# Two cross-attention layers on TensorE: the products for the running maxima issued as row tiles of 64 and of 32 rows

## The chip, the cores and the metric

The kernel runs on one core of one Trainium2 chip. Each time below is device time in microseconds (us) from one execution of the whole program; the metric is the median over runs. There is one profiled execution, and the trace belongs to it.

## The reference, cut to what matters

The program computes a small two-layer network on x (2 x 256 tokens, 256 wide) with a context of 2 x 4096 rows, 256 wide. Each layer is cross-attention over the context, a second mixer, and a feed-forward part with experts. The change touches the two cross-attentions alone:

```python
# layer 0: 8 heads of 64; layer 1: 16 heads of 16, with biases on q, k, v
q = (layernorm(x) @ Wq).reshape(b, n, HEADS, DIM_HEAD)
k = (context @ Wk).reshape(b, m, HEADS, DIM_HEAD)
v = (context @ Wv).reshape(b, m, HEADS, DIM_HEAD)
attn = softmax(q k^T * scale, axis=-1)      # over all 4096 rows of the context
x = x + (attn @ v) @ Wo + bo
```

A softmax needs a shift per query and head. The kernel takes the largest product over all 4096 keys, so it multiplies queries by keys twice: once with queries down the partitions, to reduce along the free axis to a maximum ("maxima"), and later once more with keys down the partitions, with the shift folded in, to take exponentials ("scores"). Any shift close to the maximum serves, since it cancels in the quotient.

## The kernel before, in words

**Units and chunks.** Both layers (`cross0` and `cross1`, each a function in every engine's program) work through 4 units: batch 0 or 1 times the first or second half of the heads. A unit holds 4 heads in layer 0 (`HPU0`) and 8 heads in layer 1 (`HPU1`). The 4096 rows of context are 8 chunks of 512 (`NCH`), so there are 32 chunks g in all. At step t of 41 the kernel makes keys and values of chunk t, maxima of chunk t - 1, and scores, exponentials and mixture of chunk t - 9 (`LAG` = 9, a whole unit and one step later, because the shift must be known). So steps 1 to 8 have maxima and no scores, steps 9 to 32 have both, and steps 33 to 40 have scores alone. The order on TensorE (PE) is written out by hand: for each head or block n of a step, `scores(g, n)`, then `maxima(t - 1, n)`, then the pieces that the step's plan puts there: `mixture` (attention weights times values), `keys` and `values`. PE runs its queue in order.

**Layer 1's plan (`slots_of`, L236).** There are 8 slots n in a step. In units 1 and 3 (steps 9 to 15 and 24 to 31, all but the first of the second stretch) two keys products each stand behind slots 1, 3 and 4 and the mixture behind slots 0, 2, 5 and 7; nothing stands behind slot 6 but the next scores. In unit 2 (steps 16 to 23) two keys products stand behind slot 1 and four behind slot 3, values behind 5 and 7, and the mixture behind 0, 2, 4 and 6. Step 24 and step 32 have the mixture behind 0, 2, 4 and 6 and nothing behind the odd slots.

**Layer 0's order (L1399).** Head h: `scores(g, h)` is 8 products of 256 columns, then `maxima(t - 1, h)`; behind the four heads stand keys, `mixture(g, 0)`, `mixture(g, 1)`, values and the turning of the context.

**Maxima (L1319 and L1525).** A call makes two products of 128 x 512 in fp32r for one head h: the head's queries (first 128, then last 128) are the weights, and 512 keys stream past. In layer 0 the weights are `qh0`, which holds the rounded queries twice, in partitions 0 to 63 and 64 to 127; the keys `k0` of an even head hold the rounded part in partitions 0 to 63 and the remainder in 64 to 127, an odd head the other way round. One product of 128 rows thus multiplies the queries by the whole key. In layer 1 the weights are the unit's queries masked to one head (16 rows of 128 are not zero) and `ef1` holds the rounded keys of all 8 heads of the unit.

**Where the products go.** In steps 1 to 8 (`early`) both go to one `score` tensor, two banks of PSUM, and VectorE (DVE) reduces both in one instruction (`reduce_early`, L2050). From step 9 on they go to single banks that `place_free` (L1268) hands out after waiting for the last reader, and DVE reduces each with an instruction of its own (L2085, L2210). Layer 0 rotates through three banks (`order0`, `place0`). Layer 1 has two for this: product n goes to ring place 1 + n % 2, so that product n waits for the reduction of product n - 2. `ms` counts the products done and `red` the reductions done.

**Tiles of columns.** Two existing lines issue column tiles: the mixture of layer 0 (L1344, `tile_position=(0, 64 * j)`, 64 columns of weights) and that of layer 1 (L1552, `(0, 32 * j)`, 17 columns of weights in a tile of 32). Each fp32 product there shows as two matmuls in the trace. All the other products of the two layers' loops use the array whole. No instruction of the kernel before uses a tile of rows.

The lines of the old maxima loop in layer 1, in which the wait for a bank stands ahead of each single product:

```python
for q in range(2):
    dst = score[h % 2][:, 512 * q:512 * q + 512] if early else place_free(a, g + 1, f"m{2 * h + q}")[:]
    mm(dst, masked_queries1(u)[:, h, 128 * q:128 * q + 128], ef1[:, g % ERING, 0, :], start=True, stop=True).then_inc(a["ms"], 1)
```

Of the kernel before, what the change touches and what calls it, by code (L numbers as in the profile page):

```python
# [64 lines left out]
def perceiver(nc, ins, out):  # L65
    ctx = ExitStack()
    with ctx:
# [160 lines left out]
        def masked_queries1(u):  # L228

            return qm1[:] if u % 2 == 0 else qm1b[:, :, 256:512]  # L230
# [50 lines left out]
        def bank_of(a, t, use):  # L281
            return ring[place_of(a, t, use)]
# [957 lines left out]
        def _(pe):  # L1240
# [59 lines left out]
            def cross0():  # L1300
# [17 lines left out]

                def maxima(g, h):  # L1319
                    u, i = divmod(g, NCH)  # L1320
                    if i == 0:
                        pe.wait_ge(a["qh"], a.n("qh", 8 * u + 2 * h + 2))
                    if h % 2 == 0:
                        pe.wait_ge(a["kl"], a.n("kl", 2 * g + h // 2 + 1))
                    early = g + 1 < LAG
                    if early and 4 * g + h >= 2:
                        pe.wait_ge(a["red"], a.n("red", 8 * g + 2 * h - 2))
                    for q in range(2):
                        dst = score[h % 2][:, 512 * q:512 * q + 512] if early else place_free(a, g + 1, f"m{2 * h + q}")[:]
                        mm(dst, qh0[:, u % 3, h, 128 * q:128 * q + 128], k0[:, g % LAG, h, :], start=True, stop=True).then_inc(a["ms"], 1)  # L1330

                def mixture(g, n):
                    u, i = divmod(g, NCH)
# [149 lines left out]
            def cross1():  # L1483
# [40 lines left out]

                def maxima(g, h):  # L1525
                    u, i = divmod(g, NCH)
                    if i == 0:
                        pe.wait_ge(a["qh"], a.n("qh", 8 * u + h + 1))
                    if h == 0:
                        pe.wait_ge(a["kh"], a.n("kh", g + 1))  # L1530
                    early = g + 1 < LAG
                    if early and 8 * g + h >= 2:
                        pe.wait_ge(a["red"], a.n("red", 16 * g + 2 * h - 2))
                    for q in range(2):
                        dst = score[h % 2][:, 512 * q:512 * q + 512] if early else place_free(a, g + 1, f"m{2 * h + q}")[:]
                        mm(dst, masked_queries1(u)[:, h, 128 * q:128 * q + 128], ef1[:, g % ERING, 0, :], start=True, stop=True).then_inc(a["ms"], 1)  # L1536

                def mixture(g, blocks):
                    u, i = divmod(g, NCH)
# [461 lines left out]
        def _(dve):  # L2001
# [42 lines left out]
                dve.wait_ge(a["ch"], a.n("ch", 2 * half_index(g) + f + 1))  # L2044
                v.tensor_tensor(lo[:, f, :], bank_of(a, g - 1, f"t{f}")[:], hi[:, f, :].bitcast(F32), ALU.subtract).then_inc(a["cl"], 1)

            def reduce_early(a, mx, per_chunk, g, h):

                dve.wait_ge(a["ms"], a.n("ms", per_chunk * g + 2 * h + 2))
                v.tensor_reduce(mx[:, 0, g, 2 * h:2 * h + 2], score[h % 2][:].rearrange("p (q k) -> p q k", q=2), AX.X, ALU.max).then_inc(a["red"], 2)  # L2050

            def low_weights(setup, n, lo, src, hi):

# [23 lines left out]
            def cross0():  # L2077
                a = a0

                def reduce(g, h):  # L2080
                    u, i = divmod(g, NCH)
                    for q in range(2):
                        n = 2 * h + q
                        dve.wait_ge(a["ms"], a.n("ms", 8 * g + n + 1))
                        v.tensor_reduce(mx0[:, u % 2, i, n:n + 1], bank_of(a, g + 1, f"m{n}")[:], AX.X, ALU.max).then_inc(a["red"], 1)  # L2085

                def maximum(u):
                    dve.wait_ge(a["red"], a.n("red", 8 * NCH * (u + 1)))
# [51 lines left out]
                for t in range(STEPS):  # L2140
                    g = t - LAG
                    for h in range(HPU0):
                        if LAG <= t <= CHUNKS:
                            reduce(t - 1, h)
                        if 1 <= t < LAG:
                            reduce_early(a, mx0, 8, t - 1, h)
                        if t < NCH and h in (1, 2):
                            low_keys(t, h - 1)
                    if t % NCH == 0 and 0 < t <= CHUNKS:
                        maximum(t // NCH - 1)  # L2150
                    if NCH <= t < CHUNKS:
                        low_keys(t, 0)
                        low_keys(t, 1)
                    if g > 0 and g % NCH == 0:
                        divide(a, g // NCH - 1, oT0, den0[:]).then_inc(a["o"], 1)
                    if g == CHUNKS - 1:
                        for h in (1, 2, 3):
                            last_sums(h)
                    elif g >= 0:
                        sums(g)  # L2160
                    if is_turned(t + 1):
                        context_of(t + 1)
                    if t % NCH in (1, 2, 3, 4) and t < CHUNKS:
                        low_queries(t // NCH, t % NCH - 1)
# [15 lines left out]
            def cross1():  # L2180
# [24 lines left out]
                def reduce(g, h):  # L2205
                    u, i = divmod(g, NCH)
                    for q in range(2):
                        n = 2 * h + q
                        dve.wait_ge(a["ms"], a.n("ms", 16 * g + n + 1))
                        v.tensor_reduce(mx1[:, u % 2, i, n:n + 1], bank_of(a, g + 1, f"m{n}")[:], AX.X, ALU.max).then_inc(a["red"], 1)  # L2210

                def maximum(u):
                    dve.wait_ge(a["red"], a.n("red", 16 * NCH * (u + 1)))
# [44 lines left out]
                for t in range(STEPS):  # L2258
                    g = t - LAG
                    u, i = divmod(t, NCH)  # L2260
                    for h in range(HPU1):
                        if LAG <= t <= CHUNKS:
                            reduce(t - 1, h)
                        if 1 <= t < LAG:
                            reduce_early(a, mx1, 16, t - 1, h)
                        if (t < NCH and h == 1) or ((i or u % 2 == 0) and LAG <= t < CHUNKS and h == slots_of(t)[2] + 1):
                            low_keys(t)
                        if g > NCH and t < CHUNKS:
                            finish_part(g // NCH - 1, g % NCH, h)
                    if i == 0 and 0 < t <= CHUNKS:  # L2270
                        maximum(u - 1)
                    if i == 0 and u % 2 and NCH <= t < CHUNKS:
                        low_keys(t)
                    if g > 0 and g % NCH == 0 and t > CHUNKS:
                        finish(g // NCH - 1)
                    if u and i in (1, 2, 3, 4) and t < CHUNKS:
                        low_queries(u, 2 * i - 2)
                        low_queries(u, 2 * i - 1)
                    if t == CHUNKS + 3:
                        dve.wait_ge(rw["y"], 1)  # L2280
                        v.tensor_scalar(rw_rest[:], rw_vec[:, 2:5, :], -1.0, 1.0, ALU.mult, ALU.add)
                        v.tensor_scalar(rw_wexp[:], rw_wexp[:], -1.0, None, ALU.mult).then_inc(rw["mx"], 1)
                    if CHUNKS + 2 < t < CHUNKS + 7:
                        n = t - CHUNKS - 3
                        dve.wait_ge(rw["tr"], n + 1)
                        v.tensor_copy(rw_W[:, n], bank[0][:].rearrange("p (f n) -> p f n", f=2)).then_inc(rw["trc"], 1)
# [352 lines left out]
```

## Time and profile before

| what | value |
|---|---|
| median of 3 runs | 1577.31 us (1574.79 to 1585.05) |
| the profiled execution: its own time | 1577.6 us |
| its span, first to last instruction | 1575.7 us |
| mean granted TensorE clock | 0.984 of full |
| PE busy | 1493.4 us, 95% |
| DVE busy | 1007.7 us, 64% |
| ACT busy | 757.7 us, 48% |
| POOL busy | 545.3 us, 35% |

Busy time of an engine is the time in which at least one of its instructions ran. PE's matmuls overlap in the trace, and the ends are modelled, so what one of them costs in a stream is the distance between starts, not its duration. PEld is the loading of weights, which can run beside a matmul.

### The profile page before, as it was taken

The numbers are of one execution on the slowest core, as the hardware profiler recorded it, in microseconds if no ns is written. First come the engines' busy times: TensorE is split into PE (matmuls) and PEld (weight loads), VectorE is DVE, ScalarE is ACT, GpSimd is POOL, SyncE is SP. The second block draws the span as 40 slices with busy tenths as digits, with TensorE's granted clock in tenths as the row PEclk, the third lists the DMA queues.
The fourth block names the chain that finished last, engine by engine and source line by source line (L and its number), as shares of the span: only waits on it lengthen the run. The fifth ranks groups of instructions, "written<-read, shape, count | busy, mean of one in ns | idle before, by whom it ended". The sixth has DMA issues, their size and how long they took to land.

```text
span 1575.7 us, 26268 instructions
## 1 busy us (share of the span) xinstructions
PE 1493.4 (95%) x10057; PEld 1102.0 (70%) x10057; DVE 1007.7 (64%) x1568; ACT 757.7 (48%) x1027; POOL 545.3 (35%) x688
## 2 busy tenths in 40 slices
PE   7999999999998998899999887999999999998898
PEld 6877877877886757689998664555666555444498
DVE  6976567666654367576766888876876887206711
ACT  5645555554544425443442223555555555785131
POOL 1015443452547930000000622753554554670000
PEclk9999999999999999799999999999999999999899
DMA  5433333332324200023223223211111220000354
GB/s 187 161 127 101 124 118 108 130 111 81 121 81 108 55 29 1 22 87 107 81 83 103 81 106 107 81 54 55 71 64 55 81 81 1 2 2 1 107 179 154
DMA packets 68817, 134.27 MB, mean 85 GB/s; under 512 B 9010, under 2 KB 39268, under 8 KB 68708
## 3 DMA queue, kind: packets, MB, share of 16 engines
q1 hardware_dynamic: 68516, 132.74, 25.8%
q8 instruction: 72, 1.18, 0.3%
q14 instruction: 37, 0.30, 0.1%
q10 hardware_dynamic: 192, 0.05, 0.0%
HBM read 98.64 MB, written 17.30 MB: 74 GB/s over the span
## 4 chain that ended last, share of the span: by engine, by line
PE 81%; DVE 9%; POOL 3%; ACT 2%; issue 2%; DMA 1%; SPq 1%; ACTq 0%; DVEq 0%; POOLq 0%
PE bank L1278 14%; PE score L1521 8%; PE bank L1552 8%; PE bank L1536 6%; PE bank L1842 6%; PE score L1278 6%; PE bank L1344 5%; PE bank L1330 3%; PE score L1315 3%; PE bank L1565 2%; PE score L1316 2%; DVE mx L2210 2%; DVE mx L2050 2%; PE bank L1926 2%; PE bank L1936 2%
## 5 line engine op out<-in xcount | busy, mean ns | idle before, releaser
L992 ACT ACTIVATE P<-score 128x1024 f32<-128x1024 f32 x256 | 256.5, 1024 | 145.2 <-PE score L1521 145.0
L727 POOL CAST st<-ef 32x512 fp32r<-32x512 f32 x384 | 234.9, 612 | 242.4 <-PE score L1521 197.4
L2210 DVE TENSOR_REDUCE mx<-bank 128x1 f32<-128x512 f32 x384 | 246.8, 685 | 88.5 <-PE bank L1536 84.7
L1521 PE MATMUL score<-qs,st 97*128 97x512 f32 x512 | 172.9, 426 | 3.7 <-DMA qs<-shift 2.4
L686 POOL TENSOR_TENSOR sum<-sum,P 128x512 f32<-128x512 f32 x82 | 108.5, 1324 | 185.6 <-ACT P L897 185.6
L2085 DVE TENSOR_REDUCE mx<-bank 128x1 f32<-128x512 f32 x192 | 123.7, 686 | 69.4 <-PE bank L1330 60.7
L897 ACT ACTIVATE P<-score 128x1024 f32<-128x1024 f32 x128 | 129.6, 1026 | 69.3 <-PE score L1316 67.0
L1552 PE MATMUL bank<-P,v 128*17 128x256 f32 x2048 | 134.4, 382 | 0.0
L1315 PE MATMUL score<-qh,k 128*128 128x256 f32 x512 | 130.3, 288 | 4.4 <-ACT P L897 2.3
L1521 PEld LDWEIGHTS score<-qs,st 97*128 97x128 f32 x512 | 84.3, 189 | 69.6 <-ACT P L992 36.2
L1278 PE MATMUL bank<-w_split,c_hi 128*128 128x256 f32 x688 | 128.9, 287 | 2.5 <-DVE k L2097 1.7
L1316 PE MATMUL score<-ql,w 65*128 65x256 f32 x512 | 127.9, 283 | 0.0
L1344 PE MATMUL bank<-P,v 128*64 128x256 f32 x1024 | 118.1, 382 | 0.4 <-ACT P L897 0.4
L1278 PEld LDWEIGHTS bank<-w_split,c_hi 128*128 128x128 f32 x688 | 108.0, 190 | 14.9 <-issue 8.8
L2050 DVE TENSOR_REDUCE mx<-score 128x2 f32<-128x1024 f32 x96 | 112.4, 1218 | 7.7 <-PE score L1536 4.2
L688 POOL TENSOR_TENSOR sum<-sum,P 128x512 f32<-128x512 f32 x82 | 107.9, 1316 | 6.4
L1315 PEld LDWEIGHTS score<-qh,k 128*128 128x128 f32 x512 | 97.5, 190 | 13.6 <-issue 8.6
L1536 PE MATMUL bank<-ef,qm1b 128*128 128x512 f32 x256 | 96.3, 428 | 4.0 <-DVE mx L2210 1.0
L1316 PEld LDWEIGHTS score<-ql,w 65*128 65x128 f32 x512 | 97.7, 191 | 3.2
L1344 PEld LDWEIGHTS bank<-P,v 128*64 128x64 f32 x1024 | 70.4, 137 | 42.1 <-issue 7.0
L907 ACT ACTIVATE v<-bank 128x512 f32<-128x512 f32 x64 | 38.3, 599 | 122.6 <-PE bank L1278 121.2
L1278 PE MATMUL bank<-w_split,c_lo 128*128 128x256 f32 x344 | 97.1, 282 | 0.0
(415 smaller groups left out, 2834.6 us busy)
## 6 DMA issues: line engine op xcount, KB each, us to landing
c_hi<-split_ctx SPq DMA_DIRECT2D x47, 512.0 KB, 3.2
c_lo<-split_ctx SPq DMA_DIRECT2D x47, 512.0 KB, 4.2
w<-k SPq DMA_DIRECT2D x128, 128.0 KB, 3.5
arena<-in_L_ffn_W SPq DMA_DIRECT2D x16, 1024.0 KB, 5.3
c_in<-in_ctx SPq DMA_DIRECT2D x16, 512.0 KB, 3.8
w1raw<-in_L_ffn_w SPq DMA_DIRECT2D x8, 1024.0 KB, 4.9
arena<-in_L_ffn_w SPq DMA_DIRECT2D x8, 1024.0 KB, 5.4
split_ctx<-c_hi SPq DMA_DIRECT2D x12, 512.0 KB, 3.5
```

Source lines behind the costliest of these rows:

```text
L727: pool.tensor_copy(st1[32 * block:32 * block + 32, k, :], ef1[rows, g % ERING, part, :].bitcast(F32)).then_inc(a[f"st{k}"], 16)
L897: act.activation(P[:, h, :], score[h % 2][:], ACT.Exp).then_inc(a["p"], 1)
L992: act.activation(P1[:, index % PRING, :], score[n % 2][:], ACT.Exp).then_inc(a["p"], 1)
L1278: last = mm(dst, l, r, start=(n == 0), stop=(n == len(pairs) - 1))
L1315: mm(o, k0[:, g % LAG, h, keys], qh0[:, u % 3, h, :], start=True, stop=False)
L1316: last = mm(o, w0[0:65, h, keys], ql0[0:65, u % 2, h, :], start=False, stop=True)
L1344: last = mm(mix[64 * j:64 * j + 64, S * n:S * n + S], v0[:, g % LAG, k, 64 * h:64 * h + 64], P[:, h, S * k:S * k + S], start=False, stop=F ...
L1521: last = mm(score[n % 2][:, 512 * j:512 * j + 512], st1[0:97, pair, 128 * k:128 * k + 128], qs1[0:97, u % 2, 2 * pair:2 * pair + 2, :], st ...
L1536: mm(dst, masked_queries1(u)[:, h, 128 * q:128 * q + 128], ef1[:, g % ERING, 0, :], start=True, stop=True).then_inc(a["ms"], 1)
L1552: last = mm(mix[32 * j:32 * j + 17, S * quad:S * quad + S], v1[:, (NCH * (u // 2) + i) % VRING, k, h, :], P1[:, index % PRING, S * j:S * j ...
L2050: v.tensor_reduce(mx[:, 0, g, 2 * h:2 * h + 2], score[h % 2][:].rearrange("p (q k) -> p q k", q=2), AX.X, ALU.max).then_inc(a["red"], 2)
L2210: v.tensor_reduce(mx1[:, u % 2, i, n:n + 1], bank_of(a, g + 1, f"m{n}")[:], AX.X, ALU.max).then_inc(a["red"], 1)
```

## The change

In both layers a call of `maxima` no longer makes both query halves of one head with 128 rows. It makes one query half q of two heads that lie in different groups of partitions, as two row tiles, into the same two banks.

- Layer 0: call h makes half q = h % 2 of heads 2 * (h // 2) and 2 * (h // 2) + 1. Tile j takes partitions 64 j to 64 j + 63. These rows hold the rounded keys alone, so the remainder takes no part in the maxima, and the wait is for `kh` in place of `kl`.
- Layer 1: call h makes half q = h % 2 of heads `first` and `first + 2`, in tiles of 32 rows. Rows left out are zero in the masked queries.
- Both destinations are asked for before the first product, so both waits of `place_free` stand ahead of both products.
- The waits for queries `qh` at the start of a unit ask for the later of the two heads.
- The reductions are the same in number and shape; only the column of the table of maxima to which each writes is another.

```diff
@@ PE, layer 0 @@
 def maxima(g, h):
     u, i = divmod(g, NCH)
+    pair, q = divmod(h, 2)
     if i == 0:
-        pe.wait_ge(a["qh"], a.n("qh", 8 * u + 2 * h + 2))
-    if h % 2 == 0:
-        pe.wait_ge(a["kl"], a.n("kl", 2 * g + h // 2 + 1))
+        pe.wait_ge(a["qh"], a.n("qh", 8 * u + 4 * pair + 4))
+    if q == 0:
+        pe.wait_ge(a["kh"], a.n("kh", 2 * g + pair + 1))
     early = g + 1 < LAG
     if early and 4 * g + h >= 2:
         pe.wait_ge(a["red"], a.n("red", 8 * g + 2 * h - 2))
-    for q in range(2):
-        dst = score[h % 2][:, 512 * q:512 * q + 512] if early else place_free(a, g + 1, f"m{2 * h + q}")[:]
-        mm(dst, qh0[:, u % 3, h, 128 * q:128 * q + 128], k0[:, g % LAG, h, :], start=True, stop=True).then_inc(a["ms"], 1)
+    dst = [score[h % 2][:, 512 * j:512 * j + 512] if early else place_free(a, g + 1, f"m{2 * h + j}")[:] for j in range(2)]
+    for j in range(2):
+        rows = slice(64 * j, 64 * j + 64)
+        mm(dst[j], qh0[rows, u % 3, 2 * pair + j, 128 * q:128 * q + 128], k0[rows, g % LAG, 2 * pair + j, :], start=True, stop=True,
+           tile_position=(64 * j, 0)).then_inc(a["ms"], 1)
@@ PE, layer 1 @@
 def maxima(g, h):
     u, i = divmod(g, NCH)
+    first, q = 4 * (h // 4) + h // 2 % 2, h % 2
     if i == 0:
-        pe.wait_ge(a["qh"], a.n("qh", 8 * u + h + 1))
+        pe.wait_ge(a["qh"], a.n("qh", 8 * u + first + 3))
...
-    for q in range(2):
-        dst = score[h % 2][:, 512 * q:512 * q + 512] if early else place_free(a, g + 1, f"m{2 * h + q}")[:]
-        mm(dst, masked_queries1(u)[:, h, 128 * q:128 * q + 128], ef1[:, g % ERING, 0, :], start=True, stop=True).then_inc(a["ms"], 1)
+    dst = [score[h % 2][:, 512 * j:512 * j + 512] if early else place_free(a, g + 1, f"m{2 * h + j}")[:] for j in range(2)]
+    for j in range(2):
+        head = first + 2 * j
+        rows = slice(32 * (head // 2), 32 * (head // 2) + 32)
+        mm(dst[j], masked_queries1(u)[rows, head, 128 * q:128 * q + 128], ef1[rows, g % ERING, 0, :], start=True, stop=True,
+           tile_position=(32 * (head // 2), 0)).then_inc(a["ms"], 1)
@@ DVE, layer 1; layer 0 and reduce_early alike @@
-    v.tensor_reduce(mx1[:, u % 2, i, n:n + 1], bank_of(a, g + 1, f"m{n}")[:], AX.X, ALU.max).then_inc(a["red"], 1)
+    m = 2 * (4 * (h // 4) + h // 2 % 2 + 2 * q) + h % 2
+    v.tensor_reduce(mx1[:, u % 2, i, m:m + 1], bank_of(a, g + 1, f"m{n}")[:], AX.X, ALU.max).then_inc(a["red"], 1)
```

## Rows read from the trace of the kernel before

**Rows 1.** Chain of work that ended last, by engine.

```profile
PE 81%; DVE 9%; POOL 3%; ACT 2%; issue 2%; DMA 1%; SPq 1%; ACTq 0%; DVEq 0%; POOLq 0%
```

**Rows 2.** Busy time by stretch: PE, PEld, DVE, ACT, POOL; clock, DMA, GB/s.

```profile
145.00:385.00 240.00, 236.02 (x1666) 191.99 (x1665) 154.50 (x230) 128.56 (x181) 104.74 (x83) 1.00 0.37 117
...
875.00:1000.00 125.00, 106.44 (x579) 73.10 (x581) 107.44 (x117) 38.48 (x50) 48.44 (x71) 0.97 0.28 101
...
1240.00:1370.00 130.00, 125.21 (x915) 66.75 (x915) 89.70 (x144) 80.64 (x86) 72.71 (x119) 1.00 0.09 33
```

**Rows 3.** Groups by line: the whole page's L1552; L2050 from 875 to 975 us.

```profile
L1552 PE MATMUL bank<-P,v 128*17 128x256 f32 x2048 | 134.4, 382 | 0.0
...
L2050 DVE TENSOR_REDUCE mx<-score 128x2 f32<-128x1024 f32 x64 | 74.1, 1217 | 4.6 <-PE score L1536 4.2
```

**Rows 4.** Timeline, layer 1, a step of unit 3, slot 0 to slot 0 (start, us).

```profile
1301.44 0.63 PE L1536 MATMUL bank<-ef,qm1b 128*128 128x512 f32 x2
...
1301.88 2.69 DVE L2210 TENSOR_REDUCE mx<-bank 128x1 f32<-128x512 f32 x4 [0.83 <-PE bank L1536]
...
1302.84 0.89 PE L1536 MATMUL bank<-ef,qm1b 128*128 128x512 f32 x2
...
1303.22 0.19 PEld L1536 LDWEIGHTS bank<-ef,qm1b 128*128 128x128 f32 x1 [0.41 <-DVE mx L2210]
...
1305.21 0.63 PE L1536 MATMUL bank<-ef,qm1b 128*128 128x512 f32 x2
...
1308.68 1.29 DVE L2210 TENSOR_REDUCE mx<-bank 128x1 f32<-128x512 f32 x2 [0.35 <-PE bank L1536]
...
1310.38 0.63 PE L1536 MATMUL bank<-ef,qm1b 128*128 128x512 f32 x2
...
1311.55 1.10 PE L1536 MATMUL bank<-ef,qm1b 128*128 128x512 f32 x2
...
1316.26 0.63 PE L1536 MATMUL bank<-ef,qm1b 128*128 128x512 f32 x2
```

**Rows 5.** Timeline, layer 1: into the tiles of 32 columns and out again.

```profile
1101.66 0.63 PE L1536 MATMUL bank<-ef,qm 128*128 128x512 f32 x2
...
1102.22 0.13 PEld L1552 LDWEIGHTS bank<-P,v 128*17 128x17 f32 x8 [0.37 <-issue]
1102.22 0.41 PE L1552 MATMUL bank<-P,v 128*17 128x256 f32 x4
...
1102.22 0.63 PE L1552 MATMUL bank<-P,v 128*17 128x256 f32 x8
...
1103.21 0.30 PEld L1521 LDWEIGHTS score<-qs,st 97*128 97x128 f32 x2 [0.42 <-ACT P L992]
1103.21 0.73 PE L1521 MATMUL score<-qs,st 97*128 97x512 f32 x2
...
1103.78 0.63 PE L1536 MATMUL bank<-ef,qm 128*128 128x512 f32 x2
```

**Rows 6.** Timeline, PE, layer 0: tiles of 64 columns.

```profile
303.09 0.39 PE L1278 MATMUL bank<-c_hi,w_split 128*128 128x512 f32 x1
...
303.41 0.65 PE L1344 MATMUL bank<-P,v 128*64 128x256 f32 x4
...
307.01 0.50 PE L1278 MATMUL bank<-w_split,c_hi 128*128 128x256 f32 x2
```

**Rows 7.** Chain in order of time: 96 products of 256 columns.

```profile
713.32 11.52 PE bank L1842 x96
```

**Rows 8.** Timeline, PE, unit 2 of layer 1: slot 1 of two steps; step 32.

```profile
1108.26 0.83 PE L1536 MATMUL bank<-ef,qm 128*128 128x512 f32 x2
...
1125.10 0.83 PE L1536 MATMUL bank<-ef,qm 128*128 128x512 f32 x2
...
1334.83 0.62 PE L1536 MATMUL bank<-ef,qm1b 128*128 128x512 f32 x2
...
1338.59 0.63 PE L1536 MATMUL bank<-ef,qm1b 128*128 128x512 f32 x2
```

More of the change, by code:

```diff
@@ L2045, in context_low, with reduce_early @@
                 v.tensor_tensor(lo[:, f, :], bank_of(a, g - 1, f"t{f}")[:], hi[:, f, :].bitcast(F32), ALU.subtract).then_inc(a["cl"], 1)
-            def reduce_early(a, mx, per_chunk, g, h):
+            def reduce_early(a, out, per_chunk, g, h):
                 dve.wait_ge(a["ms"], a.n("ms", per_chunk * g + 2 * h + 2))
-                v.tensor_reduce(mx[:, 0, g, 2 * h:2 * h + 2], score[h % 2][:].rearrange("p (q k) -> p q k", q=2), AX.X, ALU.max).then_inc(a["red"], 2)
+                v.tensor_reduce(out, score[h % 2][:].rearrange("p (q k) -> p q k", q=2), AX.X, ALU.max).then_inc(a["red"], 2)
             def low_weights(setup, n, lo, src, hi):
@@ L2084, in reduce @@
                         dve.wait_ge(a["ms"], a.n("ms", 8 * g + n + 1))
-                        v.tensor_reduce(mx0[:, u % 2, i, n:n + 1], bank_of(a, g + 1, f"m{n}")[:], AX.X, ALU.max).then_inc(a["red"], 1)
+                        m = 4 * (h // 2) + 2 * q + h % 2
+                        v.tensor_reduce(mx0[:, u % 2, i, m:m + 1], bank_of(a, g + 1, f"m{n}")[:], AX.X, ALU.max).then_inc(a["red"], 1)
                 def maximum(u):
@@ L2145, in cross0 @@
                         if 1 <= t < LAG:
-                            reduce_early(a, mx0, 8, t - 1, h)
+                            reduce_early(a, mx0[:, 0, t - 1, 4 * (h // 2) + h % 2:4 * (h // 2) + h % 2 + 3:2], 8, t - 1, h)
                         if t < NCH and h in (1, 2):
@@ L2264, in cross1 @@
                         if 1 <= t < LAG:
-                            reduce_early(a, mx1, 16, t - 1, h)
+                            reduce_early(a, mx1[:, 0, t - 1, 8 * (h // 4) + h % 4:8 * (h // 4) + h % 4 + 5:4], 16, t - 1, h)
                         if (t < NCH and h == 1) or ((i or u % 2 == 0) and LAG <= t < CHUNKS and h == slots_of(t)[2] + 1):
```

## The prediction

> **What bounds the kernel now.** I read the chain of waits first, then busy time by stretch, then timelines of single steps. The chain is 81% PE [rows 1], and by stretch PE is busy 236.0 of 240 us in layer 0 and 125.2 of 130 us late in layer 1 at a granted clock of 1.00 [rows 2]. So what a maxima call costs on PE is paid in full. One stretch is different: steps 1 to 8 of layer 1, where DVE is busy 107.4 us and PE 106.4 us of 125 [rows 2] and 64 reductions of 1.217 us, idle 4.6 us in all, set the pace [rows 3].
>
> The timeline of layer 1 shows a second bound under PE. A step of unit 3 takes 14.82 us from slot 0 to slot 0 (1301.44 to 1316.26) [rows 4]. Its PE work, from the pieces below, is 4 slots with mixture of 2.12, three with keys of 1.41 and one bare slot of 0.94 = 13.65 us. The missing 1.17 us are waits for the maxima banks: a pair of products takes 0.63 us undisturbed, but 0.89 and 1.10 us at 1302.84 and 1311.55, because the second needs DVE's second reduction [rows 4]. Note what saves this step today: the first product starts after the *first* reduction, so that DVE finds work and runs four reductions in 2.69 us without a gap [rows 4].
>
> **Prices from rows.**
> - A 512-column product in a stream costs 0.235 us (two take 0.63 us [rows 5], and one alone lasts 0.39 [rows 6]). A call of two is 0.47. A 256-column product costs 0.12 (96 in 11.52) [rows 7].
> - Entering a mode of column tiles: two products starting at 1101.66 would let the next start at 1102.13; it starts at 1102.22 [rows 5]. In layer 0 the one at 303.09 frees PE at 303.32 and the tile starts at 303.41 [rows 6]. Both 0.09 us, and weights are not loaded ahead: PEld starts with PE and had been idle 0.37 us [rows 5].
> - Leaving: four of the layer 1 tiles start together, the next four 0.22 later (0.41 against 0.63 for 4 and 8), so 16 take 0.88; the next product starts 0.99 after the first (1102.22 to 1103.21), 0.11 more. Then the two scores take 0.57 to the next start (1103.21 to 1103.78), not 0.47: the first must wait for its 128-column weight load, 0.10 [rows 5]. In layer 0 32 matmuls take 3.60 us (303.41 to 307.01): 16 pairs at 0.215 are 3.44, about 0.05 is the first load of 64 columns, and 0.09 to 0.11 the way out; then the first two L1278, of 256 columns, last 0.50 together, about 0.10 more than 0.12 and the 0.28 that one takes alone [rows 6]. So a change of shape is 0.09 of emptying, plus the exposed load of the next weights: nothing seen for 17 columns, 0.10 for 128.
> - Tiles of different columns do overlap fully: 4 at a time, and 2 at a time, in the time of one (0.22) [rows 5, 6]. No row shows row tiles.
>
> The Trainium skill (TensorEngine Tiling, Key Properties) says that changing the tiling mode, not merely the tile, drains TensorE; the 0.09 us of [rows 5, 6] agree for columns, and nothing here shows it for rows. By that rule the sum below stands; without it the first rival does.
>
> **Part 1: the pair as row tiles.** Removed: 0.47 us. Added: the pair together. I take 0.255: one product's 0.235 and 0.02 for the second tile, since four tiles of columns together last 0.41 where one lasts 0.382 [rows 3, 5]. Bounds: 0.235 for perfect overlap, and 0.47 for none. The second load of 128 columns may queue behind the first (0.11 apart in [rows 5]: two loads in 0.30, one lasting 0.19), which makes 0.365.
>
> **Part 2: the changes of shape.** Before and after nearly every call stands work on the whole array. In: 0.09 + 0.10 for the load of 128 columns. Out: 0.09 + 0.10. Bounds for each of the two: 0 (row tiles need no emptying) and 0.21 (the dearest seen). I take the middle values, since two kinds of column tile gave the same. An isolated call is then 0.19 + 0.255 + 0.19 = 0.635 against 0.47: **+0.165**. A call in front of a mixture (layer 1, 4 of 8) already pays the step into tiles; it gains 0.19 going in and loses 0.215: 2.095 against 2.12, **-0.025**.
>
> Layer 0, steps 9 to 32: 24 x 4 isolated calls x 0.165 = +15.8. Steps 1 to 8: 32 x 0.165 = 5.3, of which I take 5. The banks do no harm there: with three of them a call waits for the first reduction of the call before, 0.44 + 0.60 + some 0.2 us after it, and calls are 1.4 us apart or more (eight score products of 0.12 and the pair). Waiting for `kh`, not `kl`, gives nothing: mixture, values and the next scores of PE (over 8 us) lie between the keys of a chunk and its maxima.
>
> **Part 3: both bank waits ahead of both products (layer 1, steps 9 to 32).** Now the next call needs both reductions. The loop is: product start to first reduction 0.44 (1301.44 to 1301.88), two reductions 1.29 (row at 1308.68; also the first two of the 2.69), release at 1303.17 to weight load 0.05 (1303.22), load to product 0.11 (the pair of 1302.84 ends at 1303.73, so its second product, 0.39 to 0.40 long, started at 1303.33) [rows 4]. Sum **1.89 us** from call to call, whatever PE could do. Before, no such floor held for one slot; only DVE's own 0.65 per reduction did. Queued behind the waiting product on PE are the next scores, and behind them ACT and the mixture. DVE's other work, one `low_keys` and the pieces of the division, fits in the 0.6 us per slot in which DVE now idles.
>
> - Units 1 and 3, 15 steps: four slots with mixture 2.095; those with two keys products 0.255 + 0.19 + 0.47 + 0.47 + 0.19 = 1.575 and the bare one 1.105, all four raised to 1.89. Sum 15.94 against 14.82: +1.12, x 15 = +16.8.
> - Unit 2, 8 steps: period 16.84 (1108.26 to 1125.10) [rows 8]. New: four of 2.095, slot 1 at 1.89, slot 3 (four keys products) 2.045, two with values 2.545 (12 products of 0.12 = 1.44) = 17.40: +0.56, x 8 = +4.5.
> - Step 32: two slots took 3.76 (1334.83 to 1338.59) [rows 8], now 2.095 + 1.89 = 3.985: x 4, +0.9.
> - Steps 1 to 8: PE has 18 us of slack in 125 [rows 2] and waits in pairs before as now; 64 x 0.165 would be 10.6 if none were covered, 0 if all. DVE's reductions idle only 4.6 us [rows 3], so I take +2.
>
> **Other edits**, all 0: the reductions' new columns are the same work; the later `qh` wait falls at a unit's start, where those queries were made during the unit before. At the first unit it could cost one cast, under 1 us.
>
> **Sum.** 15.8 + 5 + 16.8 + 4.5 + 0.9 + 2 = +45.0 us. On the profiled execution's 1577.6 that is **1622 us**; the median of the runs is 1577.3, the same to 0.02%. The likeliest case's own range: with the loads in the way in hidden (-0.10 per call outside the 1.89 us slots: 128 in layer 0, 8 x 7 and 16 x 4 in layer 1 = 248) it is 1598; with the second load behind the first (+0.11 on the same 248) 1650.
>
> **Rivals.**
> 1. *Row tiles need no emptying and their loads run ahead.* For: nothing in the trace has a row tile, and all tiles of columns overlapped. Against: both kinds of column tile were emptied before and after. A call falls by 0.215. Layer 0: 96 x 0.215 = 20.6, and 5 of the early ones. Layer 1 keeps the 1.89 floor: units 1 and 3 four slots of 1.905 and four of 1.89 = 15.18, still +0.36 x 15 = +5.4; unit 2 four of 1.905, two of 1.89, two of 2.165 = 15.73, -1.11 x 8 = -8.9. Total -29: **1548 us**. The mechanism wins on PE once emptying and exposed load together are below (0.47 - 0.255) / 2 = 0.107 us a side; the whole 29 us come only at zero.
> The Trainium skill (TensorE: Matmul & The Clock Gate, Part 3) reports row tiles starting about 4 ns apart and a 3.07-fold gain for four of them; that bears on tiles in a row of their own, as the pair, not on the way in and out, and no row here shows it.
> 2. *The tiles do not overlap* (the change then does not do what it says), with the emptying paid. For: fp32r weights of 128 columns are a kind that no tile here has. Against: the two column tile shapes. Call +0.38 isolated, +0.19 before a mixture: layer 0 +48, units 1 and 3 16.80 against 14.82 = +29.7, unit 2 18.91 = +16.6, early and step 32 +10: **1682 us**.
> 3. *Half the price*, emptying and load together 0.10 a side: layer 0 stays as it is; units 1 and 3 are four slots of 2.005 and four of 1.89 = 15.58, +11.4 in 15 steps; unit 2 is -2.8 in all: **1587 us**.
>
> **How the numbers follow.** Forecast 0.60, rival 1 0.25, rival 2 0.07, rival 3 0.08. A measurement of this kernel can tell about 1% from no change. Rival 1 is the faster side, 0.25; rival 3, 0.6% up, is mostly within 1%, 0.06; slower 0.69. The 8 in 10 range goes from 1545, which takes in the larger part of rival 1, to 1655; rival 2 and the tails are left out.
>
> **What would show it.** Right: in layer 0 the pair of maxima products starts 0.1 to 0.2 us later than a stream would have it, both within 0.03 us, and the work behind starts late as well; in units 1 and 3 of layer 1 calls in slots 1, 3, 4 and 6 stand 1.89 us apart with DVE idle some 0.6 us before each pair; a step of unit 3 is near 15.9 us and PE's busy share there falls. Wrong: a maxima pair in layer 0 followed by the next score product within 0.26 us, weights loaded ahead of the pair, or a step of layer 0 shorter than before; then rival 1 holds. Starts of the two tiles 0.235 apart would be rival 2.

## The result, and the profile after

The changed kernel takes 1701.8 us (median of 4 runs, 1677.4 to 1760.9) against 1581.2 (4 runs). The ratio of the runs, less those that a low clock lengthened most, is 1.061, interval 1.052 to 1.070. The four runs differ as their mean granted clock does: 1677.4 us at 0.937, 1678.8 at 0.934, 1724.9 at 0.900 and 1760.9 at 0.872. The profiled one is that of 1724.9 us (span 1722.9), 147.3 us longer than the profiled one of before. The forecast, 1622 us, has the sign right and falls short by far; 1701.8 lies outside its range of 1545 to 1655.

Where the time went, by three instructions that both kernels have: the idle products ahead of the second mixer of layer 0 (end of its cross-attention), those ahead of layer 1's cross-attention, and the first denominators of layer 1, which open step 33. First the kernel before, timeline of PE:

```profile
566.65 4.06 PE L1246 MATMUL score<-zeros 128*128 128x512 bf16 x18 [1.39 <-DVEq L300]
...
862.31 4.05 PE L1246 MATMUL score<-zeros 128*128 128x512 bf16 x18
...
1346.66 1.13 PE L1588 MATMUL score<-oT,den_pick 128*128 128x256 f32 x4 [1.62 <-ACT oT L1018]
```

and the changed one:

```profile
578.15 4.06 PE L1246 MATMUL score<-zeros 128*128 128x512 bf16 x18 [1.39 <-DVEq L300]
...
875.42 4.05 PE L1246 MATMUL score<-zeros 128*128 128x512 bf16 x18
...
1494.20 1.13 PE L1595 MATMUL score<-oT,den_pick 128*128 128x256 f32 x4 [1.61 <-ACT oT L1018]
```

The stretch up to the end of layer 0's cross-attention is 11.5 us longer, what lies between 1.6, and steps 0 to 32 of layer 1 take 618.8 us for 484.4: +134.4. The remaining 75.0 us to the output products are the same in both. Busy time by stretch for those steps and for the 75 us behind them, changed kernel (columns as in [rows 2]):

```profile
875.42:1494.20 618.78, 570.73 (x3084) 280.30 (x3081) 379.62 (x551) 244.30 (x275) 239.30 (x374) 0.76 0.15 55
1494.20:1569.20 75.00, 73.68 (x664) 34.06 (x664) 7.90 (x10) 62.52 (x66) 51.78 (x84) 1.00 0.01 2
```

The same steps of the kernel before:

```profile
862.31:1346.66 484.35, 457.78 (x3085) 283.99 (x3082) 377.79 (x551) 241.02 (x275) 238.85 (x374) 0.99 0.20 70
```

The number behind the five busy times, the granted clock, is the finding: it is 0.76 over the stretch with maxima, where it was 0.99 before, and 1.00 again once they are over. DVE, ACT and POOL do the same work in the same busy time; only PE is longer busy. By level: the clock is at 2.4 GHz (a granted clock of 1.00) for some stretches and at 1.2 (0.50) for others, tens of microseconds long, in the same code. A step of units 1 and 3 in either, by the starts of its calls; first at full clock (from the call behind the bare slot, slot 7, to the next one, timeline of PE):

```profile
1086.52 0.50 PE L1542 MATMUL bank<-ef,qm1b 32*128 32x512 f32 x2 [0.81 <-DVE mx L2219]
1088.61 0.50 PE L1542 MATMUL bank<-ef,qm1b 32*128 32x512 f32 x2
1090.68 0.50 PE L1542 MATMUL bank<-ef,qm1b 32*128 32x512 f32 x2
1092.65 0.50 PE L1542 MATMUL bank<-ef,qm1b 32*128 32x512 f32 x2 [0.33 <-DVE mx L2219]
1094.73 0.50 PE L1542 MATMUL bank<-ef,qm1b 32*128 32x512 f32 x2
1096.70 0.50 PE L1542 MATMUL bank<-ef,qm1b 32*128 32x512 f32 x2 [0.33 <-DVE mx L2219]
1098.64 0.49 PE L1542 MATMUL bank<-ef,qm1b 32*128 32x512 f32 x2 [0.31 <-DVE mx L2219]
...
1102.68 0.49 PE L1542 MATMUL bank<-ef,qm1b 32*128 32x512 f32 x2 [0.81 <-DVE mx L2219]
```

then at half:

```profile
1325.59 0.79 PE L1542 MATMUL bank<-ef,qm1b 32*128 32x512 f32 x2
...
1350.89 0.79 PE L1542 MATMUL bank<-ef,qm1b 32*128 32x512 f32 x2
```

16.16 us against 25.30. Answering to [rows 4], the full-clock step is 16.16 for 14.82 before, with calls 2.07 to 2.09 apart across a mixture and 1.94 to 1.97 elsewhere, the latter held by DVE's reductions: the forecast said 15.94, 2.095 and 1.89. At half clock only one of the eight calls of the step shows a wait for DVE, and 9.1 us a step are lost. An estimate of the whole: of 618.8 us, (1 - 0.76) x 2 x 618.8 = 297 ran at half; if each gives back what it does in this step, 1 - 16.16 / 25.30 = 0.36 us, that is about 107 us. Without them the stretch would be some 512 us, 27 above before.

In layer 0 the clock is 1.00, and the price of a call can be read against [rows 5, 6] (timeline, changed kernel):

```profile
302.41 0.28 PE L1316 MATMUL score<-ql,w 65*128 65x256 f32 x1
302.62 0.19 PEld L1332 LDWEIGHTS bank<-k,qh 64*128 64x128 f32 x2
302.62 0.49 PE L1332 MATMUL bank<-k,qh 64*128 64x512 f32 x2
...
303.04 0.19 PEld L1315 LDWEIGHTS score<-qh,k 128*128 128x128 f32 x1 [0.24 <-issue]
303.04 0.39 PE L1315 MATMUL score<-qh,k 128*128 128x256 f32 x1
...
303.27 0.28 PE L1316 MATMUL score<-ql,w 65*128 65x256 f32 x1
```

The score product of 302.41 would let the next start at 302.53; the two tiles start at 302.62, 0.09 late, one with the other to the two decimals shown, and both weight loads lie inside 0.19 us. The next product is issued 0.42 later and its second 0.23 after that, 0.11 late. Whole call: 303.27 - 0.12 - 302.53 = 0.62 us for 0.47, +0.15; the forecast said +0.165. So row tiles overlap fully, loads side by side, and the array is emptied before and after, as for columns. The Trainium skill's rule (TensorEngine Tiling, Key Properties), that a change of mode drains TensorE, holds here for rows too: 0.09 us going in, and about as much going out (0.42, less 0.10 for the exposed load and 0.235 for the pair).

### The profile page after: what moved, and what is told of

Same layout as the page of the kernel before. It is cut to its first block, busy times and chain, and to the rows that moved or that the text cites. A ratio compares the mean times of both kernels' runs of the same rounds, so it can differ in the third digit from the quotient of the medians.

```text
span 1722.9 us, 26466 instructions
## 1 busy us (share of the span) xinstructions
PE 1613.9 (94%) x10057; PEld 1080.1 (63%) x10057; DVE 1010.9 (59%) x1568; ACT 760.7 (44%) x1027; POOL 544.8 (32%) x688
## 4 chain that ended last, share of the span: by engine, by line
PE 79%; DVE 11%; POOL 3%; ACT 2%; issue 2%; DMA 1%; SPq 1%; ACTq 0%; DVEq 0%; POOLq 0%
PE bank L1278 13%; PE bank L1559 9%; PE score L1524 8%; PE bank L1542 6%; PE bank L1849 5%; PE score L1278 5%; PE bank L1347 5%; DVE mx L2219 4%; PE bank L1572 3%; PE score L1315 3%; PE score L1316 2%; DVE mx L2057 2%; PE bank L1332 2%; PE bank L1933 2%; PE bank L1943 2%
## 5 line engine op out<-in xcount | busy, mean ns | idle before, releaser
L1524 PE MATMUL score<-qs,st 97*128 97x512 f32 x512 | 212.2, 509 | 3.7 <-DMA qs<-shift 2.4
L1559 PE MATMUL bank<-P,v 128*17 128x256 f32 x2048 | 172.2, 467 | 0.0
L1524 PEld LDWEIGHTS score<-qs,st 97*128 97x128 f32 x512 | 100.5, 229 | 96.2 <-issue 61.8
L1315 PE MATMUL score<-qh,k 128*128 128x256 f32 x512 | 137.6, 303 | 3.9 <-ACT P L897 2.2
L1278 PE MATMUL bank<-w_split,c_hi 128*128 128x256 f32 x688 | 136.1, 298 | 2.1 <-DVE k L2105 1.3
L1559 PEld LDWEIGHTS bank<-P,v 128*17 128x17 f32 x2048 | 53.5, 109 | 80.8 <-issue 53.3
L1542 PE MATMUL bank<-ef,qm1b 32*128 32x512 f32 x256 | 86.1, 665 | 18.5 <-DVE mx L2219 18.5
```

The lines of the kernel that those rows point to most:

```text
L1278: last = mm(dst, l, r, start=(n == 0), stop=(n == len(pairs) - 1))
L1315: mm(o, k0[:, g % LAG, h, keys], qh0[:, u % 3, h, :], start=True, stop=False)
L1524: last = mm(score[n % 2][:, 512 * j:512 * j + 512], st1[0:97, pair, 128 * k:128 * k + 128], qs1[0:97, u % 2, 2 * pair:2 * pair + 2, :], st ...
L1542: mm(dst[j], masked_queries1(u)[rows, head, 128 * q:128 * q + 128], ef1[rows, g % ERING, 0, :], start=True, stop=True, tile_position=(32 * ...
L1559: last = mm(mix[32 * j:32 * j + 17, S * quad:S * quad + S], v1[:, (NCH * (u // 2) + i) % VRING, k, h, :], P1[:, index % PRING, S * j:S * j ...
```

## The experiments

Each run was measured beside the kernel before on the same chip; the medians of that kernel are 1578.6 to 1581.0 us and its clock 0.978 to 0.985. "Clock" is the mean granted clock of each run of the kernel. The runs are spread over four chips; the comparisons below go by the difference to the kernel before on the same chip, or say otherwise.

**One layer at a time.** `e1` keeps layer 0's change and `e2` layer 1's; the other layer is that of before.

> The change in layer 0 alone; layer 1 as before. Theory W (in layer 1 PE's waits for the maxima banks let the clock fall) and theory T (in layer 1 the products on 32 of 128 rows let the clock fall) expect the same here: the stretch up to the end of layer 0 is 17 us longer, as in the changed kernel, so about 1595 us, and the mean granted clock stays near the 0.98 of before. A clock well below that would say that the 64-row tiles alone can bring it down.

> The change in layer 1 alone; layer 0 as before. Both theories: all of the half clock comes from here, so mean clock about 0.93 and about 1660 us (the 1678 of the undisturbed runs of the changed kernel less the 17 of layer 0), with a wide spread between runs.

Layer 0 alone: 1593.6 us (1586.3 to 1597.5), ratio 1.0093 (1.0074 to 1.0112), clock 0.980 to 0.984. Layer 1 alone: 1728.6 us (1693.9 to 1748.3), clock 0.874 to 0.909. Run again on another chip (`e2b`, expectation with the third tile below) it was 1696.0 us (1654.3 to 1714.3), clock 0.897 to 0.946. All of the lost clock is layer 1's; 64-row tiles in layer 0 do not touch it.

**Waits or tiles?** `e3` has the new order and both waits, without tiles:

```diff
-mm(dst[j], masked_queries1(u)[rows, head, ...], ef1[rows, ...], ..., tile_position=(32 * (head // 2), 0))
+mm(dst[j], masked_queries1(u)[:, head, ...], ef1[:, ...], ...)
```

> Layer 1 alone, with the new pairs of heads and both bank waits ahead of both products, but each product on the whole array as before. The floor from call to call is 1.89 us, so units 1 and 3 are 16.0 us a step against 14.8, and unit 2 some 0.3 more: +21 us at a full clock, 1598 us. Theory W: PE waits as long as in the changed kernel, so the clock falls too, to 0.93 to 0.95, and the time is 1630 us or more. Theory T: the clock stays at 0.98 and the time at about 1598 us.

`e4` has the 32-row tiles, with `place_free` back in the loop ahead of each product.

> Layer 1 alone, with 32-row tiles, but each product behind its own bank wait as before the change. DVE is fed as before, so that PE waits little; what stays is the price of changing the array's shape. At a full clock units 1 and 3 are 15.0 to 15.6 us a step: 1585 to 1595 us. Theory W: clock 0.98 and that time. Theory T: the clock falls as in the changed kernel, 0.93 or so, and the time is over 1630 us.

`e3`: 1610.5 us (1607.4 to 1619.9), ratio 1.021 (1.018 to 1.025), clock 0.980 to 0.984. `e4`: 1660.2 us (1633.9 to 1676.5), clock 0.919 to 0.947. Theory W fell and theory T stood. PE waits as much in `e3` as in the changed kernel and keeps its clock. Steps 0 to 32 of layer 1, the stretch of 618.8 us and clock 0.76 above, in `e3`:

```profile
857.89:1376.65 518.76, 458.95 (x3084) 280.26 (x3082) 379.59 (x551) 241.19 (x275) 238.22 (x374) 0.99 0.18 66
```

PE is busy 88% there, less than in the changed kernel (92%), at a clock of 0.99. In `e4` it hardly waits and loses the clock: from 1000 to 1340 us it is busy 335.8 of 340 us at 0.91. The waits are not without weight, though: on the same chip the 32-row tiles had 0.919 to 0.947 with own waits (`e4`) and 0.874 to 0.909 with both ahead (`e2`). They lower the clock where the tiles are, and not without them.

`e3` also prices the waits: some 30 us, not the 21 of its expectation. Its timeline shows where part of that comes from (PE):

```profile
1302.60 0.70 PE L1538 MATMUL bank<-ef,qm1b 128*128 128x512 f32 x2 [0.32 <-DVE mx L2214]
1304.80 0.63 PE L1538 MATMUL bank<-ef,qm1b 128*128 128x512 f32 x2
1306.66 0.70 PE L1538 MATMUL bank<-ef,qm1b 128*128 128x512 f32 x2 [0.77 <-DVE mx L2214]
1308.86 0.63 PE L1538 MATMUL bank<-ef,qm1b 128*128 128x512 f32 x2
1311.37 0.70 PE L1538 MATMUL bank<-ef,qm1b 128*128 128x512 f32 x2 [0.23 <-DVE mx L2214]
...
1323.38 0.70 PE L1538 MATMUL bank<-ef,qm1b 128*128 128x512 f32 x2 [0.77 <-DVE mx L2214]
```

The floor is as forecast, 1.86 to 1.94 us from call to call; a slot with mixture that follows a wait is 2.20, not 2.12, since the pair itself lasts 0.70 for 0.63. The step is 16.72 us (1306.66 to 1323.38) where I had 16.04, and 0.39 of the 0.68 lie in one slot, 2.51 us (1308.86 to 1311.37) for 2.12: there DVE does 1.42 us of other work (`low_queries`, L2205, from 1308.49) between two pairs of reductions. Steps without it take 16.24. By the starts of slot 0 in both traces, the 15 steps of units 1 and 3 are 27 us longer than before (18 expected) and unit 2 is 6 us longer (2.4 expected); that execution reached layer 1 4 us earlier, so 30 us remain.

**The order alone.** `e11` is `e3` with each product behind its own wait.

> Layer 1 alone, the new pairs of heads only: whole-array products, each behind its own wait. Nothing but the order of the heads differs from the kernel before: 1575 to 1583 us, clock 0.98. The run with both waits ahead differs from this one by the place of the waits alone, so the difference (about 30 us) is the price of that.

1579.5 us (10 runs), ratio 0.9997 (0.9968 to 1.0026). So the new order costs nothing, and the 30 us of `e3` are due to the place of the waits, the only thing in which the two differ.

**Rows or emptying?** `e5` uses 64-row tiles in layer 1 (heads `h // 2` and `h // 2 + 4` in place of `first` and `first + 2`). `e7` is `e3` with a tiny 32-row product behind each call from step 9 on, in 7 of 8 steps:

```diff
 maxima(t - 1, n)
+if g % NCH:
+    mm(mix[:, 0:8], zeros[0:32, :], zeros[0:32, 0:8], start=False, stop=False, ..., tile_position=(0, 0))
```

> Layer 1 alone, tiles of 64 rows instead of 32 (heads h and h + 4), both waits ahead. Calls, waits, emptying and loads are the same in number as with 32-row tiles; only the rows that a product drives are doubled. Theory R (it is the few rows in use during the maxima that let the clock fall): clock clearly above the 0.89 of the 32-row run, 0.94 to 0.98, and 1605 to 1650 us. Theory E (it is the emptying of the array 8 times more often a step): clock as with 32 rows, 0.87 to 0.91, and 1690 us or more.

> Whole-array products with both waits ahead (the run at 1610 us and 0.98), plus one product of zeros on 32 rows and 8 columns behind each call in 7 of 8 steps: it brings the emptying of the array and the exposed load of weights, without taking rows from the maxima. By the prices from the rows (0.19 in, 0.19 out, the tiny product 0.03 to 0.1) calls in front of a mixture get 0.2 longer and the others end inside the 1.89 us floor or just above it: +25 to +45 us on the 1610 at a full clock, 1635 to 1655. Theory E: the clock falls to 0.94 or less and the time is above 1670 us. Theory R: the clock stays at 0.98.

`e5`: 1619.1 us (1608.8 to 1625.6), ratio 1.023 (1.017 to 1.028), clock 0.973 to 0.980. `e7`: 1621.8 us (1621.0 to 1627.5), ratio 1.028 (1.025 to 1.031), clock 0.982 to 0.984. Theory E fell: changing the array's shape eight times a step, tiny product included, costs 11 to 14 us over `e3`, less than expected, and no clock. That is not the price of the tiles in layer 1, since in `e7` the pair itself is not halved. Twice the rows in a tile bring the clock back nearly whole: with the same number of calls and waits `e5` is 77 us shorter than `e2b` and 110 shorter than `e2`, by the medians. Those ran on other chips; on the chip of `e5`, `e8` below (the 32-row kernel and 8 us of extra products) took 1656.4 and 1713.6 us at 0.948 and 0.910.

**Fillers.** `e6` adds whole-array products of zeros where PE waits; its edit is below. `e9` issues the first score product again in the same slots:

```diff
 scores(g, n)
+if t <= CHUNKS and g % NCH and not (n in (0, 2) or n in slots_of(t)[1]):
+    for _ in range(2 if n == 6 else 1):
+        mm(mix[:, 0:512], zeros[:], bc(zeros[:], 1, 4), start=False, stop=False, ...)
```

> Layer 1 alone with 32-row tiles, and one product of zeros over the whole array (two in the bare slot) ahead of the bank wait in slots without mixture, where PE would wait 0.3 to 0.8 us; they add zero to the running mixture. If the clock depends on how much of the array works over a stretch, whatever the work is, it rises from 0.89 to 0.94 or more and the time falls below 1660 us although instructions are added; at a full clock the fillers cost little, since they lie in the wait (1600 to 1615 us). If it depends on the maxima products themselves alone, clock and time stay as in the 32-row run, 0.87 to 0.91 and 1694 to 1748 us.

> Layer 1 alone with 32-row tiles, as the filled run, but the filler is not a product of zeros: in the same slots the first score product is issued once more (twice more in the bare slot) and overwritten by the right one. If zeros were the reason why the fillers did not bring the clock back, real operands do: clock 0.95 or more, under 1650 us. If it is the tiles themselves (or PE's stops beside them), it stays as with zeros: clock 0.90 to 0.95 between runs, 1665 to 1730 us.

`e6`: 1706.8 us (1665.0 to 1731.2), clock 0.899 to 0.951. `e9`: 1678.5 us (1668.2 to 1702.5), clock 0.919 to 0.943. Neither came under the 1650 to 1660 us that would have spoken for fillers, though one run of `e6` had a clock of 0.951. Their clocks cover about the range of the 32-row kernel without fillers (0.874 to 0.948 in `e2`, `e2b` and `e8`), and so do their times, less what the fillers themselves add: little or no help that these runs can tell, and no difference between zeros and real data.

**A burst.** `e8` puts 36 such products at the start of step 34.

> Layer 1 alone with 32-row tiles, and 36 products of zeros on the whole array at the start of step 34, after the last maxima. Steps 33 to 40 hold no maxima and ran at a clock of 1.00 before the change, but mostly at 0.50 after it. If the half clock only carries over from the steps with tiles, the 8 us of dense work put it back and it stays at 1.00 to the end of layer 1, some 25 to 35 us less in that stretch. If those steps by themselves can't hold the full clock once layer 1 is slower, the clock falls again within some 10 us and the stretch keeps its length.

1656.4 and 1713.6 us. Its premise was wrong: I had placed steps 33 to 40 about 100 us too early in the trace. They run at 1.00 in the changed kernel as well (the 75 us above), so the burst tests nothing; the run only serves as one more of the 32-row kernel, on the chip of `e5`, `e6` and `e7`.

**A third tile.** `e13` adds, beside each pair in 7 of 8 steps from step 9 on, a product on 32 rows that the pair leaves idle:

```diff
+if j == 0 and not early and (g + 1 - LAG) % NCH:
+    free = slice(64 - 64 * (h // 4), 96 - 64 * (h // 4))
+    mm(mix[:, 0:512], masked_queries1(u)[free, head, ...], ef1[free, ...], start=False, ...,
+       tile_position=(64 - 64 * (h // 4), 0))
```

> Layer 1 alone with 32-row tiles and both waits ahead, and in 7 of 8 steps from step 9 on a third 32-row product beside each pair, on rows that the pair leaves idle, with real keys and zero weights, added to the mixture's bank. Number of mode changes, waits and shape of the tiles are those of the 32-row run; 96 rows are in use during a call instead of 64. If it is the rows in use during the maxima, the clock rises well above the 0.89 of that run, 0.94 to 0.97, and the time falls to 1620 to 1665 us. If it is the 32-row shape by itself, clock and time stay at 0.87 to 0.91 and 1694 to 1748 us. If the third tile does not overlap, it adds about 0.24 us a call, 40 us in all, to either.

> The 32-row run once more, on the same chip as the third tile, since its clock differs from execution to execution: 1690 to 1750 us and 0.87 to 0.91 again. If it is nearer to 1660, the ranges expected of the third tile shift with it.

1640.4 us (1632.2 to 1645.3), clock 0.949 to 0.959; the same kernel without it, beside it on the chip, 1696.0 (1654.3 to 1714.3) and 0.897 to 0.946. Work was added and 56 us went, in medians. All three tiles run at once (timeline of PE, third tile is L1543):

```profile
1182.90 0.49 PE L1539 MATMUL bank<-ef,qm 32*128 32x512 f32 x1
1182.90 0.50 PE L1543 MATMUL bank<-ef,qm 32*128 32x512 f32 x1
1182.91 0.50 PE L1539 MATMUL bank<-ef,qm 32*128 32x512 f32 x1
```

and the busy time by stretch, ahead of step 9 (no third tile in either) and behind it, first `e13`:

```profile
870.00:970.00 100.00, 85.24 (x392) 56.64 (x390) 81.58 (x80) 18.38 (x30) 32.55 (x44) 0.83 0.29 105
1000.00:1340.00 340.00, 309.42 (x2283) 155.61 (x2284) 234.33 (x370) 177.33 (x193) 166.97 (x267) 0.96 0.16 60
```

then `e2b`:

```profile
870.00:970.00 100.00, 83.68 (x396) 56.37 (x396) 81.84 (x81) 18.94 (x31) 32.53 (x44) 0.86 0.29 105
1000.00:1340.00 340.00, 319.34 (x1965) 154.47 (x1964) 210.54 (x331) 161.28 (x176) 153.64 (x245) 0.83 0.15 53
```

The clock differs only where the third tile is: 0.96 against 0.83. This profile of `e2b` is of its longest run, 0.897 over the whole; the four runs of `e13` (0.949 to 0.959) lie above the four of `e2b` (0.897 to 0.946), but the best of `e2b` comes close. With shape, waits and mode changes equal, this speaks for the rows in use during the calls. The third product is also work added, in itself a rival; the whole-array work that `e6` and `e9` added outside the calls did not do the same.

**Tiles in steps 1 to 8 alone.** `e14` is `e4` with whole-array products once `early` is over.

> Layer 1 alone, each product behind its own wait: 32-row tiles in steps 1 to 8 only, whole-array products from step 9 on. With tiles everywhere this form took 1634 to 1677 us. If each stretch answers for its own clock, the half clock is confined to about 870 to 970 us, where DVE sets the pace and covers part of it: 1580 to 1600 us, clock 0.96 to 0.98. If a half clock once begun carries itself on, it lasts beyond step 9 and the time is over 1620 us.

1587.8 us (10 runs), ratio 1.006 (1.003 to 1.009), clock 0.966 to 0.973. Its stretches:

```profile
870.00:970.00 100.00, 85.80 (x412) 57.68 (x410) 80.68 (x83) 19.00 (x31) 32.73 (x45) 0.86 0.28 99
1000.00:1340.00 340.00, 335.17 (x2395) 201.36 (x2388) 260.23 (x413) 196.84 (x215) 183.16 (x294) 1.00 0.18 63
```

The half clock ends soon after the tiles: the last tiles start at 973.13, and from 990 us on the clock is 1.00. With tiles up to step 32 (`e4`) it is 0.91 over the second stretch. A stretch answers for its own clock.

**What a better form would be worth.** `e10` has 64-row tiles with own waits in layer 1, `e12` the change in both layers with 64 rows in layer 1.

> Layer 1 alone, 64-row tiles, each product behind its own bank wait: the change of shape alone, without the floor from both waits and with the clock nearly kept. 32-row tiles with own waits, set back to the half-clock time of the kernel before by the slope of their four runs, come to about 1584 us; so 1583 to 1597 us at a clock of 0.97 or more, and some 25 us less than the 64-row run with both waits ahead (1619).

> The change in both layers with 64-row tiles in layer 1 in place of 32. If the parts add up: 1579 + 13 to 15 (layer 0) + 40 (layer 1 with 64 rows) = 1632 us, clock 0.97; 45 us or more below the fastest run of the change, all of it by the clock.

`e10`: 1600.0 us (1595.5 to 1603.5), ratio 1.012 (1.009 to 1.015), clock 0.975 to 0.981. `e12`: 1635.6 us (1634.8 to 1639.2), ratio 1.036 (1.033 to 1.039), clock 0.970 to 0.974. The parts add up: 13 (`e1`) + 41 (`e5`) = 54, and `e12` is 56 above its before. Not all of the 56 are terms at full clock; steps 0 to 32 of layer 1 in `e12`:

```profile
871.17:1403.10 531.93, 466.68 (x3085) 242.15 (x3082) 379.45 (x551) 243.44 (x275) 237.98 (x374) 0.95 0.18 64
```

The clock is 0.95 where it was 0.99 before. By the same estimate as above, with 0.36 us given back for each at half clock, some 15 of the 56 us are clock. No run with tiles came out below the kernel before: with tiles in layer 1, own waits and nearly the full clock (`e10`) are still 20 us slower.

## Why the prediction was wrong

- **The change of shape (Part 2) held.** 0.62 us a call against 0.635, by the steps predicted: emptying, exposed load, overlapped pair, emptying, exposed load. Rivals 1, 2 and 3 fell on that reading. (Rival 3's sum for unit 2 has a slip: with slot 3 raised to the 1.89 floor it is -2.5, not -2.8.)
- **Layer 0** was put at +20.8 and came to about +13 (`e1`) to +14. From step 9 on the sum is nearly right: from the first score product, 98.85 before and 96.60 after, to the end, 467.8 and 481.6 us, +13.8 for 15.8. The 5 us of steps 1 to 8 did not come: from the first maxima to that score product it is 67.1 us before and 67.0 after. Calls 0 and 1 stand next to each other there and share one way in and out: from the product ahead of them to the one behind, 0.89 us (67.91 to 68.80) for 1.07 before (70.20 to 71.27).

Layer 0's opening in the kernel before (PE): the first maxima, a step, and the first score product:

```profile
31.74 1.09 PE L1330 MATMUL score<-k,qh 128*128 128x512 f32 x4
...
70.20 0.28 PE L1278 MATMUL bank<-w_split,c_lo 128*128 128x256 f32 x1
70.32 1.09 PE L1330 MATMUL score<-k,qh 128*128 128x512 f32 x4
71.27 0.50 PE L1278 MATMUL bank<-c_first_hi,w_split 128*128 128x512 f32 x1
...
98.85 0.28 PE L1315 MATMUL score<-qh,k 128*128 128x256 f32 x1
```

and in the changed one:

```profile
29.59 0.73 PE L1332 MATMUL score<-k,qh 64*128 64x512 f32 x4
...
67.91 0.28 PE L1278 MATMUL bank<-w_split,c_lo 128*128 128x256 f32 x1
68.12 0.73 PE L1332 MATMUL score<-k,qh 64*128 64x512 f32 x4
68.80 0.50 PE L1278 MATMUL bank<-c_first_hi,w_split 128*128 128x512 f32 x1
...
96.60 0.28 PE L1315 MATMUL score<-qh,k 128*128 128x256 f32 x1
```

- **Both waits ahead (Part 3)** was the right mechanism, mis-sized. The waits alone cost 30 us (`e3` against `e11`), where the sum held 24 for the waits and the tiles of layer 1 together. A slot with mixture became longer on whole-array products, 2.20 for 2.12, and DVE's `low_queries`, 1.42 us between slots 0 and 1 of a step, were not in the sum. The tiles add little to it at full clock: the run of `e5` at a clock of 0.980 takes 1608.8 us, 30 above its before, as `e3` does.
- **The step that failed** is the one not in the sum: the clock. I read a granted clock of 1.00 [rows 2] and carried it over ("what a maxima call costs on PE is paid in full"), pricing PE's work after the change at the rate of before; none of the rivals had another clock either. What the runs show in its place is a clock of 0.76 over steps 0 to 32 of layer 1, from the 32-row tiles: 0.98 with the same waits and whole-array products (`e3`), 0.874 to 0.946 with the tiles (`e2`, `e2b`), 0.973 to 0.980 with 64 rows (`e5`). The terms at full clock are some 13 us in layer 0 (`e1`) and 30 in layer 1 (`e3`), 43 together against the 45 forecast. That they meet is in part luck: layer 0 was put 8 us too high and layer 1 6 us too low. The rest, some 50 us in the shortest run and 140 in the longest, is PE at 1.2 GHz in layer 1.
- **What stays open.** The runs show that wider tiles or a third one, both of which put more rows to use during a call, bring the clock back, and that DVE waits and mode changes by themselves do not take it. That the rows in use are what counts is the simplest reading of them, not a proof. They do not show why whole-array fillers a few tenths of a us before the call did so little, why waits and tiles together cost more clock than tiles alone, nor why the same kernel ranged from 0.87 to 0.95 between executions.

## What to carry to other kernels

Row tiles among whole-array work pay for their way in and out each time: 0.19 us a side with 128 columns of weights, so that a pair of 512-column products, saving 0.215, does not earn it; two such pairs back to back did, by 0.18 us. Two producers into two banks must keep each its own wait, or one reader turns into a lock-step loop (30 us here, for moving one wait by one line). And a PE-bound kernel's forecast needs a case in which the clock differs: look at how many rows of the array the new instructions drive, not only at how busy the engine is.

## What was not expected of the hardware

- A stretch in which PE was busy 92% of the time (570.7 of 618.8 us) had a granted clock of 0.76; before the change, 95% busy (457.8 of 484.4) had 0.99, and `e3`, only 88% busy (459.0 of 518.8), had 0.99 too. Busy share does not tell them apart; 32-row tiles in place of whole-array products do. The Trainium skill (TensorE: Matmul & The Clock Gate, Part 1) says that the clock follows how busy the engine has been; these runs add that of two loads the one with the higher busy share in the profile can get the lower clock.
- Masked weights do not matter to it: in `e3` 112 of 128 weight rows are zero and the clock is 0.98.
- Weight loads of two row tiles run side by side, two of 128 columns within 0.19 us, where two whole-array loads take 0.30 [rows 5].
